# Gated cross-attention stack on one core: 16-column heads with scores formed twice

## The chip, the cores and the metric

The kernel runs on one core of a Trainium2 chip. The metric is the device time of one execution in microseconds, the median of several runs.

## The reference, cut to what matters

Four layers, each of a cross-attention and a mixture-of-experts feed-forward, work on x of shape 8 x 256 x 256 (batches, tokens, columns). The layers att1 and att2 are the ones that matter here: x is normalized, and with the context (8 x 256 x 256) it gives q, k and v of 16 heads of 16 columns. For each batch and head

```
scores = (q @ k.T) / 4 + mask        # 256 x 256
p      = softmax(scores)             # over the keys
head   = p @ v                       # 256 x 16
x      = x + tanh(g) * (concat(heads) @ Wo + bo)
```

att1 also rotates q and k (rotary positions) and is causal. In att1 the mask of keys is all ones in the data; in att2 it blanks some keys. Everything is float32. The kernel splits numbers in a rounded part (fp32r, "hi") and a remainder ("lo") where it uses the fast fp32r products: three products (hi hi, hi lo, lo hi) make one exact enough.

## The kernel before, in words

`build_program` (L2019) runs the layers one after the other; each phase ends with a barrier of all engines. `attention_layer` (L1705) calls `heads_phase` (L1032) for att1 and att2 with 16-column heads (`small`), and for att3 with 64-column heads.

A batch has 256 tokens, two tiles of 128 rows. All engines walk the same schedule: a loop over the batches (`run_loop`, the first and the last batch written out), and in it 16 slots, one for each head. In slot h, PE (L1254 to L1394) issues `scores` of head h+3, `turn_p` of head h, the rounds of this slot and `values` of head h-2:

- `scores` (L1255): a bf16 product (L1268) puts the mask in the PSUM bank, then two fp32r products of 256 columns (L1273) add q k, one for each tile of tokens. q and k are laid out in 64 rows a head, as hi and lo parts side by side, so that one product gives all parts.
- DVE takes the minimum of the negated scores (`max_of`, L1506), ACT forms the exponential with the row's minimum as its bias and sums the row (L1405), DVE inverts the sum (L1510), POOL multiplies the 128x512 weights by it (L1623).
- `turn_p` (L1280) turns the four 128x128 blocks of the weights on PE (L1284). ACT copies them to fp32r (L1412), DVE forms the remainder (L1514).
- `values` (L1287): four fp32r products of 256 columns (L1302). The stationary block has v of four heads in its columns, hi and lo, zeros elsewhere; four heads share a bank.
- `project` (L1315): the outputs of the batch, 512 rows by hi and lo, times Wo, 24 products.

The rounds prepare the next batch in two further PSUM banks: nT (turn of the normalized x, L1333), q, k, v (12 products each through `mm3`, L92, lines L94 to L96), and four rounds each of turning the laid-out q and k (L1355). POOL normalizes x (L1638, L1640), and for att1 rotates q and k (L1655 to L1663) and multiplies q by `kq` (L1666). ACT lays out the hi parts (L1436), DVE the lo parts (L1573). SP loads the next batch's context (L1244) when the v products are through. The bias is added by POOL (L1671) after DVE's L1529.

Before the loop, `load_split` (L975) runs a block of its own: DVE computes the statistics and builds the mask of every batch (L1134 to L1146), POOL clears `vp` (L1160).

## Time and profile before

| what | us |
|---|---|
| median of 3 runs | 3881.68 (3880.99 to 3884.53) |
| span of the profiled execution, first to last instruction | 3798.7 |
| median less span | 83.0 |
| PE, DVE, ACT, POOL busy | 2830.3, 2787.6, 1844.2, 1914.3 |
| mean granted TensorE clock | 0.892 of 2.4 GHz |
| att1, att2 (start to the start of the next phase) | about 412, 364 |

The profile is of one execution; its own total with launch and end is not shown beside the span. The page gives the span, each engine's busy time, the span in 40 slices, the DMA queues, the chain of work that ended last and the costliest groups by line. A group says what was written and read, shapes, count, busy time, mean ns of one, and what ended the engine's idle time before it. On PE the records of products overlap (each has a drain at its end), so the distance of two starts is what one costs.

### The profile page before, as it was taken

What the parts mean: (1) busy time and instruction counts of PE and PEld (TensorE: products, weight loads), DVE (VectorE), ACT (ScalarE), POOL (GpSimd) and SP (SyncE); (2) the same over time, 40 slices, a digit from 0 to 9 for tenths busy, and PEclk for the clock granted to TensorE, in tenths of its full rate; (3) what the DMA queues carried; (4) which work ended last, traced back from release to release, by engine and by line L of the source; (5) the groups of instructions that cost most, each with busy time, mean ns of one, the idle gap of its engine ahead of it and who ended that gap; (6) DMA issues with size and microseconds to landing.
All of it is one profiled execution on the core that took longest, in us unless ns stands there. A gap on an engine that the chain in (4) does not pass through costs nothing. (4 is left out here: it accounts for less than half of the span.)

```text
span 3798.7 us, 69506 instructions
## 1 busy us (share of the span) xinstructions
PE 2830.3 (75%) x20444; PEld 2544.2 (67%) x20480; DVE 2787.6 (73%) x5350; ACT 1844.2 (49%) x4487; POOL 1914.3 (50%) x1464
## 2 busy tenths in 40 slices
PE   5663683488969999749992588888179999598883
PEld 4562572377749999737771477777078988498883
DVE  4665697577758999868784588898656676588886
ACT  3222352266645555437772244444256666465551
POOL 0102656466623688745552666666434433227775
PEclk9786896589989999969996799999589999799997
DMA  3043685100007656420000455554300000275654
GB/s 96 17 139 121 225 248 161 41 12 17 6 28 261 210 190 208 157 72 12 11 6 29 149 156 158 158 155 129 100 8 12 6 11 6 96 238 183 188 179 131
DMA packets 244101, 410.95 MB, mean 108 GB/s; under 512 B 25952, under 2 KB 135660, under 8 KB 243680
## 3 DMA queue, kind: packets, MB, share of 16 engines
q1 hardware_dynamic: 230112, 371.43, 30.8%
q0 software_dynamic: 13824, 37.53, 3.1%
q8 instruction: 78, 1.28, 0.1%
q14 instruction: 87, 0.71, 0.1%
HBM read 330.72 MB, written 78.38 MB: 108 GB/s over the span
## 5 line engine op out<-in xcount | busy, mean ns | idle before, releaser
L1623 POOL TENSOR_TENSOR att_p<-att_p,att_ri 128x512 f32<-128x512 f32 x384 | 416.9, 1088 | 600.6 <-DVE att_ri L1510 596.7
L500 POOL TENSOR_TENSOR moe2m_wlo<-moe2m_raw,moe2m_whi 128x768 fp32r<-128x768 f32 x184 | 343.4, 1867 | 199.2 <-ACT moe2m_whi L623 166.2
L1405 ACT ACTIVATE att_p<-att_s,att_nm 128x256 f32<-128x256 f32 x768 | 357.9, 477 | 39.3 <-DVE att_nm L1506 37.9
L1514 DVE TENSOR_TENSOR att_pTlo<-att_t,att_pThi 128x512 fp32r<-128x512 f32 x384 | 263.8, 687 | 107.9 <-ACT att_pThi L1412 106.0
L500 POOL TENSOR_TENSOR moe1m_wlo<-moe1m_raw,moe1m_whi 128x768 fp32r<-128x768 f32 x138 | 273.3, 1987 | 128.7 <-ACT moe1m_whi L623 128.7
L1506 DVE TENSOR_REDUCE att_nm<-att_s 128x2 f32<-128x512 f32 x384 | 261.5, 681 | 93.9 <-PE att_s L96 45.5
L500 POOL TENSOR_TENSOR moe3m_wlo<-moe3m_raw,moe3m_whi 128x512 fp32r<-128x512 f32 x184 | 249.1, 1370 | 138.1 <-ACT moe3m_whi L623 124.7
L717 DVE TENSOR_TENSOR moe2m_hlo<-moe2m_h_f,moe2m_hhi 128x256 fp32r<-128x256 f32 x184 | 302.5, 1644 | 13.9 <-issue 0.3
L1412 ACT ACTIVATE att_pThi<-att_t 128x512 fp32r<-128x512 f32 x384 | 230.8, 601 | 157.0 <-PE att_t L1284 153.9
L1284 PE MATMUL att_t<-g_ident,att_p 128*128 128x128 f32 x1536 | 254.9, 290 | 19.6 <-POOL att_p L1623 18.3
L587 POOL DMA_INDIRECT rows_x<-moe_n_all,moe_slot_w x144 | 151.5, 1052 | 220.1 <-POOLq L109 118.0
L94 PE MATMUL moe1m_gu<-moe1m_xThi,moe1m_whi 128*128 128x256 f32 x744 | 213.7, 287 | 7.7 <-DVE moe1m_xTlo L677 7.7
L717 DVE TENSOR_TENSOR moe3m_hlo<-moe3m_act,moe3m_hhi 128x256 fp32r<-128x256 f32 x248 | 201.1, 811 | 19.6 <-issue 1.3
L651 ACT ACTIVATE moe2m_act<-moe2m_gu 128x256 f32<-128x256 f32 x184 | 70.5, 383 | 296.9 <-PE moe2m_gu L96 296.9
L1284 PEld LDWEIGHTS att_t<-g_ident,att_p 128*128 128x128 f32 x1536 | 171.4, 144 | 61.5 <-POOL att_p L1623 27.9
L94 PE MATMUL moe2m_gu<-moe2m_xThi,moe2m_whi 128*128 128x256 f32 x736 | 210.9, 287 | 1.4 <-DVE moe2m_xTlo L677 1.4
L95 PE MATMUL moe1m_gu<-moe1m_xTlo,moe1m_whi 128*128 128x256 f32 x744 | 210.9, 284 | 0.0
L96 PE MATMUL moe1m_gu<-moe1m_xThi,moe1m_wlo 128*128 128x256 f32 x744 | 210.5, 283 | 0.0
L95 PE MATMUL moe2m_gu<-moe2m_xTlo,moe2m_whi 128*128 128x256 f32 x736 | 208.9, 284 | 0.0
L96 PE MATMUL moe2m_gu<-moe2m_xThi,moe2m_wlo 128*128 128x256 f32 x736 | 208.3, 283 | 0.0
L623 ACT ACTIVATE moe1m_whi<-moe1m_raw 128x768 fp32r<-128x768 f32 x186 | 157.6, 847 | 96.6 <-PE moe1m_yp L96 75.3
L94 PE MATMUL moe2m_yp<-moe2m_whi,moe2m_hhi 128*128 128x256 f32 x368 | 121.5, 330 | 92.0 <-DVE moe2m_hlo L717 91.4
(591 smaller groups left out, 11209.0 us busy)
## 6 DMA issues: line engine op xcount, KB each, us to landing
moe1m_raw<-in_moe_w SPq DMA_DIRECT2D x186, 384.0 KB, 4.4
moe2m_raw<-in_moe_w SPq DMA_DIRECT2D x184, 384.0 KB, 3.1
moe3m_raw<-in_moe_w SPq DMA_DIRECT2D x248, 256.0 KB, 3.5
moe0m_raw<-in_moe_w SPq DMA_DIRECT2D x92, 320.5 KB, 3.5
rows_x<-att_zeros SPq DMA_DIRECT2D x24, 512.0 KB, 6.5
...
```

What stands on the lines that cost most here:

```text
L94: pe.matmul(out, lhs[0], rhs[0], start=first, stop=False, **kw)
L95: pe.matmul(out, lhs[0], rhs[1], start=False, stop=False, **kw)
L96: return pe.matmul(out, lhs[1], rhs[0], start=False, stop=last, **kw)
L500: e.tensor_tensor(wlo[s][:, :], raw[s][:, 0:WW], whi[s][:, :].bitcast(F32), ALU.subtract).then_inc(w_lo_v if in_shared(i, lo, hi, c // FC) ...
L623: act.activation(whi[s][:, :], raw[s][:, 0:WW], ACT.Copy).then_inc(w_hi, 1)
L717: v.tensor_tensor(hh[1][q][:, :], h_f[q][:, :], hh[0][q][:, :].bitcast(F32), ALU.subtract).then_inc(h_ready, 1)
L1284: mm = pe.transpose(t_ps[s % 2][:, kc, t * P:(t + 1) * P], p_sb[s % 4][:, t, kc * P:(kc + 1) * P], ident[:, :])
L1405: ins = act.activation(p_sb[s % 4][:, t, :], src[:, t, :], ACT.Exp, bias=nm[:, s % 4, t:t + 1], scale=-1.0, accum_out=rs[:, s % 4, t:t + 1])
L1412: act.activation(pT[0][s % 4][:, :, :], t_ps[s % 2][:, :, :], ACT.Copy).then_inc(ph_done, 1)
L1506: v.tensor_reduce(nm[:, s % 4, :], s_ps[s % 2][:, :, :], AX.X, ALU.min).then_inc(m_ready, 1)
L1514: v.tensor_tensor(pT[1][s % 4][:, :, :], t_ps[s % 2][:, :, :], pT[0][s % 4][:, :, :].bitcast(F32), ALU.subtract).then_inc(pl_done, 1)
L1623: pool.tensor_tensor(p_sb[s % 4][:, :, :], p_sb[s % 4][:, :, :], ri[:, s % 4, :].rearrange("p (t o) -> p t o", o=1).broadcast_to([P, TB, S ...
```

## The change

att1 and att2 get a function of their own, `small_phase`. Each head's scores are formed twice. The straight ones (`scores`, eight slots ahead) serve only to find the largest of each row (`largest` on DVE). The maxima of four heads are turned on PE (round "mt"), negated by ACT and written by two small transfers of SP into row 49 (and 113) of the laid-out q, opposite to a row of ones in k. The turned scores (`shifted`: k is stationary, q streams) then come out less the maximum; ACT's exponential (`weights_of`) writes the weights turned, into one of four fp32 buffers. `values`, two heads behind, has a weight block as stationary operand and streams 17 columns of v, the last of them ones, as a plain fp32 product; the 17th column of the result is the row's sum. `normalize` divides eight heads at a time and OT is turned on PE. q of every second head is laid out in the other 64 rows, with zeros in the rest, so the products use all 128 rows. In att1 only three of the four blocks of a head are formed (`QB` 384), the causal mask is a product of 128x128 bf16 constants, and rows that see no key get their weights by a product with `ind`. The mask of keys is a column beside the laid-out k. The loop over the batches is written out in all engines. Wo is no longer doubled (`OC` 2).

```diff
@@ lay_out, head_weights @@
-    out["L1_Wo"], out["L2_Wo"] = twice(tr(a["L1_xattn_Wo"])), twice(a["L2_xattn_Wo"])
-    out["mask2"] = a["mask_Bx1xS2_ik0"].reshape(B, S)
+    out["L1_Wo"], out["L2_Wo"] = np.ascontiguousarray(tr(a["L1_xattn_Wo"])), a["L2_xattn_Wo"]
+    by_token = lambda m: np.ascontiguousarray(m.reshape(B * TB, P).T)
+    out["mask1"], out["mask2"] = by_token(a["mask_BxS2_if1"]), by_token(a["mask_Bx1xS2_ik0"])
-    HD, OC = 16 * dh, 4 if dh == 16 else 8
+    HD, OC = 16 * dh, 2 if dh == 16 else 8
@@ new function @@
+def small_phase(nc, G, I, name, layer, weights, w, mask, biases, rotary):
+    H, dh, L = 16, 16, 8
+    NS = B * H
+    scale = 0.25
+    NEG = -1.0e9 if rotary else -BIG
+    QB = 384 if rotary else 512
+    MC = 3 if rotary else 2
+
+    plan = [(-4, "nT", 0), (-3, "q", 0), (-2, "k", 0), (1, "v", 0), (3, "qT", 0), (5, "kT", 0), (6, "qT", 1), (7, "kT", 1),
+            (8, "qT", 2), (10, "kT", 2), (11, "qT", 3), (15, "kT", 3), (13, "mt", 0), (17, "mt", 1), (21, "mt", 2), (25, "mt", 3),
+            (27, "OT", 0), (35, "OT", 1), (37, "out", 0)]
+    ROUNDS = sorted(((16 * (b - 1) + at, kind, b, part) for b in range(B) for at, kind, part in plan), key=lambda r: r[0])
+    POS = {r[1:]: i for i, r in enumerate(ROUNDS)}
...
+    def rounds_at(s):
+        return [r[1:] for r in ROUNDS if r[0] == s]
...
+        qs, ks = (sb(n, [P, TB, H, 4, dh], F32R) for n in ("qs", "ks"))
+        QT = [sb(f"QT{q}", [P, 2, H // 2, S], F32R) for q in range(2)]
+        KT = [sb(f"KT{q}", [P, H // 2, S], F32R) for q in range(2)]
+        vp = [sb(f"vp{q}", [P, KC, H, dh + 1]) for q in range(2)]
+        p_sb = [sb(f"p{q}", [P, QB]) for q in range(4)]
...
+                for s in range(FIRST, LAST):
+                    for kind, b, part in rounds_at(s):
+                        if kind == "mt":
+                            n = 4 * b + part
+                            sp.wait_ge(mt_done, n + 1)
+                            for e in range(2):
+                                sp.dma_start(QT[b % 2][64 * e + 49:64 * e + 50, e, 2 * part:2 * part + 2, :].bitcast(F32),
+                                             mT[n % 2][4 * e:4 * e + 4, :].bitcast(F32)).then_inc(row_in, 16)
+                        if kind == "v" and b < B - 1:
+                            load_c(b + 1)
...
+                def scores(s):
+                    b, h = divmod(s, H)
+                    j = h // 4
+                    if h % 4 == 0:
+                        pe.wait_ge(rd_act, done("qT", b, j))
+                        pe.wait_ge(rd_dve, done("kT", b, j))
+                    if s == H:
+                        pe.wait_ge(cleared, 2)
+                    if s >= 2:
+                        pe.wait_ge(m_done, s - 1)
+                    bank, q, k = s_ps[s % 2], QT[b % 2], KT[b % 2]
+                    if rotary:
+                        pe.matmul(bank[:, P:3 * P], ident16[:, :], tri[:, :, :], start=True, stop=False, skip_group_check=True)
+                        pe.matmul(bank[:, 0:2 * P], q[:, h % 2, h // 2, 0:P], k[:, h // 2, :], start=False, stop=False, skip_group_check=True)
+                        mm = pe.matmul(bank[:, 2 * P:3 * P], q[:, h % 2, h // 2, P:S], k[:, h // 2, 0:P], start=False, stop=True, skip_group_check=True)
+                    else:
+                        for t in range(TB):
+                            mm = pe.matmul(bank[:, t * S:(t + 1) * S], q[:, h % 2, h // 2, t * P:(t + 1) * P], k[:, h // 2, :], start=(t == 0), stop=True,
+                                           skip_group_check=True)
+                    mm.then_inc(s_ready, 1)
+
+                def shifted(s):
+                    b, h = divmod(s, H)
+                    if h % 4 == 0:
+                        pe.wait_ge(row_in, 32 * (4 * b + h // 4 + 1))
+                    if s >= 2:
+                        pe.wait_ge(e_done, s - 1)
+                    bank, q, k = t_ps[s % 2], QT[b % 2], KT[b % 2]
+                    if rotary:
+                        if s == 0:
+                            pe.wait_ge(dg_done, 1)
+                        pe.matmul(bank[:, P:3 * P], tri[:, 0, :], dg[:, b, :, :], start=True, stop=False, skip_group_check=True)
+                        pe.matmul(bank[:, 0:S], k[:, h // 2, 0:P], q[:, h % 2, h // 2, :], start=False, stop=False, skip_group_check=True)
+                        mm = pe.matmul(bank[:, S:S + P], k[:, h // 2, P:S], q[:, h % 2, h // 2, 0:P], start=False, stop=True, skip_group_check=True)
+                    else:
+                        for c in range(KC):
+                            mm = pe.matmul(bank[:, c * S:(c + 1) * S], k[:, h // 2, c * P:(c + 1) * P], q[:, h % 2, h // 2, :], start=(c == 0), stop=True,
+                                           skip_group_check=True)
+                    mm.then_inc(st_ready, 1)
+
+                def values(s):
+                    b, h = divmod(s, H)
+                    g, half = h % 8, s // 8
+                    if h == 0:
+                        pe.wait_ge(rd_dve, done("v", b))
+                    if g == 0 and half >= 2:
+                        pe.wait_ge(on_done, half - 1)
+                    out = o_ps[half % 2][:, 0:16 * (dh + 1)].rearrange("p (t h c) -> p t h c", t=2, h=8)
+                    v = vp[b % 2]
+                    if rotary and g == 0:
+                        if s == 0:
+                            pe.wait_ge(ind_done, 2)
+                        pe.matmul(out[:, 1, :, :], ind[:, b, :], v[:, 1, 8 * (h // 8):8 * (h // 8) + 8, :], start=True, stop=False, skip_group_check=True)
+                    pe.wait_ge(e_done, s + 1)
+                    p = p_sb[s % 4]
+                    if rotary:
+                        blocks = [(0, 0, 0), (1, 0, P), (0, 1, 2 * P)]
+                    else:
+                        blocks = [(t, c, c * S + t * P) for c in range(KC) for t in range(TB)]
+                    for i, (t, c, at) in enumerate(blocks):
+                        mm = pe.matmul(out[:, t, g, :], p[:, at:at + P], v[:, c, h, :], start=(not rotary and g == 0 and i == 0),
+                                       stop=(i == len(blocks) - 1), skip_group_check=True)
+                    mm.then_inc(pv_done, 1)
+
...
+                    elif kind in ("qT", "kT"):
+                        if part == 0:
+                            pe.wait_ge(aux_done, b + 1)
+                            pe.wait_ge(laid_lo, 2 * b + 1 + (kind == "kT"))
+                        flat = (qs if kind == "qT" else ks)[:, :, :, :, :].rearrange("p t h g d -> p t (h g d)")
+                        for c in range(2):
+                            for t in range(TB):
+                                at = c * S + (1 - t if kind == "qT" else t) * P
+                                mm = pe.transpose(bank[:, at:at + P].bitcast(F32R), flat[:, t, (2 * part + c) * P:(2 * part + c + 1) * P], identr[:, :])
+                    elif kind == "mt":
+                        n = 4 * b + part
+                        pe.wait_ge(mq_ready, n + 1)
+                        mm = pe.transpose(bank[0:8, 0:P], mm_sb[n % 2][:, :, :, :].rearrange("p e a t -> p (e a t)"), ident[:, :])
...
+                pe.wait_ge(cleared, 1)
+                for s in range(FIRST, max(LAST, NS + 3)):
+                    if rotary and s == -7:
+                        pe.wait_ge(dg_done, 1)
+                        for q in range(2):
+                            pe.matmul(o_ps[q][:, :], G["ones_bf"][:, :], dgc[:, 4 * q:4 * q + 4, :], start=True, stop=True).then_inc(ind_ready, 1)
+                    if 0 <= s + L < NS:
+                        scores(s + L)
+                    if 0 <= s < NS:
+                        shifted(s)
+                    for r in rounds_at(s):
+                        round_(*r)
+                    if 0 <= s - 2 < NS:
+                        values(s - 2)
...
+                def weights_of(s):
+                    act.wait_ge(st_ready, s + 1)
+                    if s >= 4:
+                        act.wait_ge(pv_done, s - 3)
+                    act.activation(p_sb[s % 4][:, :], t_ps[s % 2][:, 0:QB], ACT.Exp).then_inc(e_done, 1)
+
+                def lay_hi(b, kind):
+                    f, dst = (qf, qs) if kind == "q" else (kf, ks)
+                    act.wait_ge(f_ready, 2 * b + 1 + (kind == "k"))
+                    if b > 0:
+                        act.wait_ge(rd_ready, POS[(kind + "T", b - 1, 3)] + 1)
+                    src = f[:, :, :].rearrange("p t (h d) -> p (t h) d", d=dh)
+                    flat = dst[:, :, :, :, :].rearrange("p t h g d -> p (t h) g d")
+                    src = src.rearrange("p n (o d) -> p n o d", o=1).broadcast_to([P, TB * H, 2, dh])
+                    act.activation(flat[:, :, 0:2, :] if kind == "q" else flat[:, :, 0:3:2, :], src, ACT.Copy).then_inc(laid_hi, 1)
...
+                    elif kind == "qT":
+                        act.wait_ge(rd_ready, pos + 1)
+                        if b >= 2:
+                            act.wait_ge(st_ready, 16 * (b - 2) + 4 * part + 4)
+                        for e in range(2):
+                            ins = act.activation(QT[b % 2][64 * e:64 * e + 64, e, 2 * part:2 * part + 2, :], both(bank)[64 * e:64 * e + 64], ACT.Copy)
+                        ins.then_inc(rd_act, 1)
+                    elif kind == "mt":
+                        n = 4 * b + part
+                        act.wait_ge(rd_ready, pos + 1)
+                        if n >= 2:
+                            act.wait_ge(row_in, 32 * (n - 1))
+                        act.activation(mT[n % 2][:, :], bank[0:8, 0:P], ACT.Copy, scale=-1.0)
+                        act.drain().then_inc(mt_done, 1)
+                        act.drain().then_inc(rd_act, 1)
...
+                def largest(s):
+                    b, h = divmod(s, H)
+                    n, e, a = s // 4, h % 2, h % 4 // 2
+                    v.wait_ge(s_ready, s + 1)
+                    if h % 4 == (3 if rotary else 0) and n >= 2:
+                        v.wait_ge(rd_ready, POS[("mt", (n - 2) // 4, (n - 2) % 4)] + 1)
+                    m = m3 if rotary else mm_sb[n % 2]
+                    v.tensor_reduce(m[:, e, a, :], s_ps[s % 2][:, 0:QB].rearrange("p (c k) -> p c k", c=MC), AX.X, ALU.max).then_inc(m_done, 1)
+                    if h % 4 == 3:
+                        if rotary:
+                            v.drain()
+                            v.tensor_tensor(mm_sb[n % 2][:, :, :, 0], m3[:, :, :, 0], m3[:, :, :, 1], ALU.max)
+                            v.tensor_copy(mm_sb[n % 2][:, :, :, 1], m3[:, :, :, 2])
+                        v.drain().then_inc(mq_ready, 1)
+
+                def lay_lo(b, kind):
+                    f, dst = (qf, qs) if kind == "q" else (kf, ks)
+                    v.wait_ge(laid_hi, 2 * b + 1 + (kind == "k"))
+                    src = f[:, :, :].rearrange("p t (h d) -> p (t h) d", d=dh)
+                    flat = dst[:, :, :, :, :].rearrange("p t h g d -> p (t h) g d")
+                    lo, hi = (2, 0) if kind == "q" else (1, 0)
+                    v.tensor_tensor(flat[:, :, lo, :], src, flat[:, :, hi, :].bitcast(F32), ALU.subtract).then_inc(laid_lo, 1)
...
+                def normalize(half):
+                    b, g = divmod(half, 2)
+                    v.wait_ge(pv_done, 8 * half + 8)
+                    if half >= 2:
+                        v.wait_ge(rd_ready, POS[("OT", b - 1, g)] + 1)
+                    o = o_ps[half % 2][:, 0:16 * (dh + 1)].rearrange("p (n c) -> p n c", c=dh + 1)
+                    v.reciprocal(ri[:, :], o[:, :, dh])
+                    v.drain()
+                    out = o_sb[:, :, g * P:(g + 1) * P].rearrange("p t (h d) -> p t h d", d=dh)
+                    o4 = o_ps[half % 2][:, 0:16 * (dh + 1)].rearrange("p (t h c) -> p t h c", t=2, h=8)
+                    r4 = ri[:, :].rearrange("p (t h o) -> p t h o", t=2, o=1).broadcast_to([P, 2, 8, dh])
+                    v.tensor_tensor(out, o4[:, :, :, 0:dh], r4, ALU.mult).then_inc(on_done, 1)
...
+                def aux(b):
+                    if b > 0:
+                        pool.wait_ge(rd_ready, POS[("kT", b - 1, 3)] + 1)
+                    for t in range(TB):
+                        cols = lambda y: y[:, TB * b + t:TB * b + t + 1].broadcast_to([P, H])
+                        if rotary:
+                            pool.tensor_copy(qs[:, t, :, 3, 0], kq[:, b, t:t + 1].broadcast_to([P, H]))
+                        pool.tensor_copy(ks[:, t, :, 3, 0], cols(km))
+                    pool.drain().then_inc(aux_done, 1)
...
+                def clear(q):
+                    for e in range(2):
+                        pool.drain()
+                        pool.memset(QT[q][64 - 64 * e:128 - 64 * e, e, :, :].bitcast(F32), 0.0)
...
+                pool.wait_ge(stats, 1)
+                norm(0)
+                clear(0)
+                pool.drain().then_inc(cleared, 1)
+                pool.wait_ge(kq_done, 1)
+                for b in range(B):
+                    if b > 0:
+                        norm(b)
+                    aux(b)
+                    if rotary:
+                        rotate(b, "q")
+                        rotate(b, "k")
+                    if b == 0:
+                        clear(1)
+                        pool.drain().then_inc(cleared, 1)
+                    if b >= 2:
+                        add_bias(b - 2)
...
@@ attention_layer @@
-        heads_phase(nc, G, I, "att1", 1, 16, head_sources(I, 1), w, mask=I["mask_BxS2_if1"], rotary=True,
-                    biases=(I["L1_bq"], I["L1_bk"], I["L1_bv"]))
+        small_phase(nc, G, I, "att1", 1, head_sources(I, 1), w, I["mask1"], (I["L1_bq"], I["L1_bk"], I["L1_bv"]), True)
     if layer == 2:
-        heads_phase(nc, G, I, "att2", 2, 16, head_sources(I, 2), w, mask=I["mask2"],
-                    biases=(I["L2_xattn_bq"], I["L2_xattn_bk"], I["L2_xattn_bv"]))
+        small_phase(nc, G, I, "att2", 2, head_sources(I, 2), w, I["mask2"], (I["L2_xattn_bq"], I["L2_xattn_bk"], I["L2_xattn_bv"]), False)
     if layer == 3:
```

## Rows read from the trace of the kernel before

**Rows 1.** Windows of att1 and att2: stretch, busy us (instructions) of each engine, PEclk, DMA, GB/s

```profile
680.00:1092.00 412.00, 337.08 (x2140) 276.07 (x2176) 283.05 (x612) 250.47 (x800) 237.90 (x225) 0.87 0.05 15
1641.00:2005.00 364.00, 325.81 (x2176) 262.69 (x2176) 276.07 (x601) 251.14 (x801) 176.05 (x153) 0.93 0.05 16
```

**Rows 2.** Timeline of SP: issues of the context loads, two of att1, two of att2

```profile
765.02 0.35 SPq L1244 DMA_DIRECT2D att_cT_hi<-ctxT_hi  x1
...
991.50 0.33 SPq L1244 DMA_DIRECT2D att_cT_hi<-ctxT_hi  x1
...
1704.76 0.34 SPq L1244 DMA_DIRECT2D att_cT_hi<-ctxT_hi  x1
...
1909.54 0.33 SPq L1244 DMA_DIRECT2D att_cT_hi<-ctxT_hi  x1
```

**Rows 3.** Timeline of PE, one head of att2: start, us covered, line, operation

```profile
1695.59 0.39 PE L1268 MATMUL att_s<-att_mask,att_ident 128*128 128x512 bf16 x1
...
1696.34 0.66 PE L1284 MATMUL att_t<-g_ident,att_p 128*128 128x128 f32 x4
1696.75 0.37 PE L1302 MATMUL att_o<-att_pThi,att_vp 128*128 128x256 f32 x1
1696.96 0.28 PE L1302 MATMUL att_o<-att_pTlo,att_vp 128*128 128x256 f32 x1
1697.08 0.28 PE L1302 MATMUL att_o<-att_pThi,att_vp 128*128 128x256 f32 x1
...
1697.32 0.39 PE L1268 MATMUL att_s<-att_mask,att_ident 128*128 128x512 bf16 x1
```

**Rows 4.** Timeline of PE in att1: four turns of laid-out q

```profile
993.33 0.54 PE L1355 MATMUL att_r<-g_identr,att_qs 128*128 128x128 f32 x4
```

**Rows 5.** Groups of att2 by line and shape: count, busy us, mean ns, idle before

```profile
L1506 DVE TENSOR_REDUCE att_nm<-att_s 128x2 f32<-128x512 f32 x128 | 87.0, 680 | 22.8 <-PE att_s L1273 19.5 <-issue 2.6 <-ACT att_p L1405 0.6
...
L1412 ACT ACTIVATE att_pThi<-att_t 128x512 fp32r<-128x512 f32 x128 | 77.1, 602 | 43.4 <-PE att_t L1284 41.4
```

**Rows 6.** Timeline of PE in the router of the second expert phase (fp32 products, turns)

```profile
1105.28 3.60 PE L274 MATMUL moe1r_lgp<-moe1r_nT,moe1r_rw 128*8 128x512 f32 x8
1108.81 0.41 PE L280 MATMUL moe1r_small<-g_ident,moe1r_lgT 8*128 8x8 f32 x4
```

**Rows 7.** Timeline of the start of att1

```profile
680.51 4.36 POOL L1160 MEMSET att_vp<- 128x5120 f32 x1 [8.86 <-POOLq L109]
...
690.65 2.77 DVE L1141 TENSOR_TENSOR att_mask<-att1p_causal,att1p_row 128x512 bf16<-128x512 bf16 x8
693.49 4.42 DVE L1144 TENSOR_REDUCE att_kq<-att_mask 128x16 f32<-128x4096 bf16 x1
...
701.68 1.12 PE L1333 MATMUL att_r<-g_ident,att_n 128*128 128x128 f32 x4 [96.20 <-POOLq L1647]
...
707.97 1.29 POOL L1655 TENSOR_TENSOR att_turn<-att_qf,att_cs 128x512 f32<-128x512 f32 x1 [6.47 <-DVEq L1545]
...
713.23 1.06 ACT L1436 ACTIVATE att_qs<-att_qf 128x1024 fp32r<-128x1024 f32 x1 [9.80 <-POOL att_qf L1666]
...
729.60 0.79 PE L1273 MATMUL att_s<-att_KT,att_QT 64*128 64x256 f32 x2 [0.38 <-DVE att_QT L1555]
```

**Rows 8.** Timeline of PE: the wait of att1 behind the rotation of q

```profile
1031.03 0.61 PE L1268 MATMUL att_s<-att_mask,att_ident 128*128 x1 [3.23 <-ACT att_p L1405]
```

**Rows 9.** Timeline of PE: start of att2

```profile
1655.28 1.12 PE L1333 MATMUL att_r<-g_ident,att_n 128*128 128x128 f32 x4 [62.95 <-POOLq L1647]
...
1672.99 0.65 PE L1268 MATMUL att_s<-att_mask,att_ident 128*128 128x512 bf16 x1
```

**Rows 10.** The context load by its line: issue to landing, us

```profile
DMA to landing us min/median/max: 2.5/2.8/3.2
```

**Rows 11.** Windows of a start of att2 and of an end of att1 (as rows 1)

```profile
1680.00:1688.00 8.00, 8.00 (x29) 5.55 (x29) 4.76 (x10) 4.92 (x17) 5.87 (x6) 0.50 0.01 2
1062.00:1082.00 20.00, 18.02 (x119) 13.96 (x119) 15.58 (x36) 16.53 (x55) 11.72 (x12) 1.00 0.01 1
```

261 lines of the change are left out of this document (259 added, 2 removed).

## The prediction

> **What bounds the kernel now.** I read the windows of the two phases first. The change touches only the two attention phases with 16-column heads: att1 (rotary, causal), about 412 us, and att2, about 364 us [rows 1]. In both, PE has work for 80 to 90% of the time, DVE and ACT for two thirds, so no engine waits for memory; the loads of the context are two per batch. Those loads mark the batches, because the next one is issued when the v projection is through: five batches of att1 take 991.50 - 765.02 = 226.5 us, 45.3 each, five of att2 1909.54 - 1704.76 = 204.8 us, 41.0 each [rows 2].
>
> Then the PE timeline of one warm head in att2 [rows 3]. It goes from mask to mask in 1697.32 - 1695.59 = 1.73 us: the bf16 mask product and the two score products 0.75, the four turns of the weights 0.41, the four value products 0.57. Back-to-back products of 256 columns are 0.12 apart (1696.96 to 1697.08); the first after turns costs 0.21, so a switch of kind costs about 0.09. Sixteen heads are 27.7 us. A round of four fp32r turns covers 0.54, of which the drain of the last is 0.16 (0.28 long at a pitch of 0.12), so it holds PE for 0.38 [rows 4]. Rounds of a batch now: nT 0.4, q, k, v 36 x 0.12 = 4.3, eight turns 3.0, output 24 x 0.12 = 2.9, together 10.6. Work of PE: 38.3 of 41.0 us. So att2 is bound by PE; att1 adds about 4 us of waits.
>
> **The change, part by part.** *Removed per head:* on PE the mask product, the four turns (0.41) and the four wide value products (0.57); on ACT two exponentials with their accumulator reads and the copy of 0.60; on DVE the subtraction of 0.69 and the reciprocal; on POOL the normalization. *Kept:* the maximum, 0.68 us on DVE; ACT now does one exponential of 128x512 from PSUM, for which I take the copy of that shape, 0.60 [rows 5]. PE now writes the scores twice, straight and turned.
>
> *Scores in att2:* 4 x 0.12 = 0.48. *Values:* four fp32 products of 17 columns with a full stationary block. The trace has no such thing. The nearest: an fp32 product appears as two records (the router's 8 records in 3.60 us are four products, 0.43 a record for 512 columns, two cycles a column) [rows 6]. So each value product is two loads and two short streams. The same group has four fp32 loads of 128 columns, each followed by 8 columns: 0.41 us in all, less 0.16 of drain, 0.06 each; without taking off the drain 0.10. I take 0.07, near the lower end since 17 columns at two cycles are 14 ns. Eight of them: 0.56, with bounds 0.48 and 0.83. The Trainium skill (TensorE: Matmul & The Clock Gate, LDWEIGHTS) puts a load at columns/1.2 ns, 107 ns for 128; by it the eight would be 0.86. The row above, 0.10 at most, speaks against it. A head is then 0.48 + 0.56 + 0.09 (one switch) = 1.13, sixteen 18.1 us.
>
> *Rounds:* output 12 products instead of 24 (1.4), OT turns 0.4, mt turns 0.4, the rest as before: 9.5, and 0.9 for ten switches: 10.4. Sum 28.5. The gap between work and batch is 2.7 us now; v no longer waits behind the doubled layout on DVE, so I keep 2.1: **30.6 us a batch in att2**. The cover is good: ACT has 16 x 0.60 + about 9.9 (the four qT copies in two halves 4.8, layouts 2.1, the rest 3) = 19.5; DVE 16 x 0.68 + about 10.5 = 21.4.
>
> *att1:* each set of scores is a bf16 product of 256 columns (0.11), one fp32r of 256 (0.12) and one of 128 (0.10): 0.65 for both. Values 6 x 0.07 = 0.42, the product for empty rows 0.03, three switches 0.3: 1.40 a head, 22.4 the batch, with rounds 32.8. Now a stall. POOL fills the auxiliary columns for batch b only when kT of batch b-1 is through, one slot before ACT lays out q. The q rotation takes from 707.97 to 713.23, 5.2 us, and k one multiplication less, about 4.2 [rows 7]. With the fill it is 6 us after the start of that slot, and ACT wants it after about 2. Behind that wait on ACT sit the next exponentials, behind the layout on DVE the maxima, and PE's scores wait for those. Counting on through both layouts PE loses about 3.4 us a batch. Now it loses 3.2 in one such wait and the clock falls after it [rows 8]; I add 3 us for that: **39.2 us a batch in att1**.
>
> *Prologue of att1:* the mask operations on DVE go (2.77 and 4.42 us), and with them a block boundary and casts, some 2 us; PE would start its first turns at 692.5 instead of 701.68. Added: zeroing half of QT before PE may start. The memset of 5120 columns takes 4.36, so 2 x 2048 take 3.5; in att1 that lies beside DVE's small mask operations and costs nothing, in att2, where DVE has less to lose, it costs what the boundary gives. Rotation, layouts and eight heads' scores ahead of the first turned ones put slot 0 at about 725; now the first scores are at 729.60 [rows 7]. att2: PE starts at 1655.28 and has scores at 1672.99 [rows 9]; then follow eight heads' scores, the next batch's nT, q and k and the first maxima, so slot 0 comes at about 1681.
>
> *The row of maxima:* PE turn, ACT copy and drain, then two small transfers of SP. A load of the context lands 2.5 to 3.2 us after issue [rows 10]; for 2 KB I take 2.0 (bounds 1.5 and 3.2). In all about 3.7 us; from the turn to the first use there are two and a half slots with their rounds, 4.3 or more. Cost nothing; if late, 1 us four times a batch.
>
> **The sum.** att1: 45 + 7 x 39.2 + last batch 25 (16 x 1.40 and 2.8 of rounds) + tail 7 = 351, now 412: -61. att2: 40 + 7 x 30.6 + 21 + 7 = 282, now 364: -82. Four small weight blocks less in the two preceding expert phases cost and give nothing, they lie beside the gathers. The span 3798.7 us becomes 3656; the median 3881.68 is 83 us more than the span (launch and end, the profiled execution's own total isn't shown), so 3739, rounded **3740 us**.
>
> **Rivals.** *Loads bound the values.* A stationary load is not hidden and a pair costs 0.104 as in the turns (four in 0.41) [rows 3]. Then +0.27 a head in att2 and +0.20 in att1: 128 x 0.47 = 60 us, 3800. This is what the skill's LDWEIGHTS rule says as well. For: the load has nothing long to hide behind. Against: rows 6. Chance 0.15.
>
> *Late row of maxima, or waits at each hand-over:* four waits of 1 us in 16 batches, 64 us: 3804. For: SP issues in order, two transfers each. Against: the distance in slots. Chance 0.13.
>
> *Everything better hidden:* no switches, no stall: batches of 26.5 and 31 us, -29 and -57: 3655. Against: switches are in the rows, and the wait for the rotation too. Chance 0.12.
>
> *Slower: the clock.* In 1680 to 1688 PE is busy for 8.00 of 8.00 us and the granted clock stays 0.50 (1.2 GHz), with many turns in the mix; in 1062 to 1082 it is 1.00 (2.4 GHz) [rows 11]. The skill (same page, PE-mode transpose) says that turns don't count as busy for the gate; the first row fits, and by that rule dropping them costs nothing. But value products that are mostly loading may weigh as little. At half clock a head of att2 is 4 x 0.21 + 8 x 0.14 + 0.1 = 2.1 us and its rounds about 17: 51 a batch, +20; att1 +18. Over all batches 38 x 7.5 = 285 us, 4025. It decides from half: 143 of 285. I put the case at 0.65 of the time: +185, 3925. For: about 45% of a warm head streams columns, where now 46% does beside the turns, so it is close. Against: q, k, v and output are dense and bring it back. Chance 0.12.
>
> **Numbers.** Forecast case 0.48, its own range 3690 to 3790. The range takes in all but the clock case: 3640 to 3860. About 0.2% (8 us) can be told from no change. Faster 0.87 (all but the clock case and a little), within 0.2% 0.02, slower 0.11.
>
> **What would show it.** Right: batches of 31 and 39 us between context loads; fp32 value records about 0.07 apart; POOL in att1 ending its rotation while ACT waits in the layout; clock near 1.0 in att2. Wrong: value pairs at 0.10; PE waiting for the row's DMA; a granted clock of 0.5 between the dense rounds; a batch of att1 over 45.

## The result, and the profile after

The changed kernel takes 3955.15 us (median of 4 runs, 3950.98 to 3963.29) where the kernel before takes 3881.34 in the same set: ratio 1.0196, 95% interval 1.0181 to 1.021. It is 74 us slower; the forecast was 3740. (Of the experiments below, one of the four executions of turned_stand_longer took 5655.61 us, for a reason that nothing here shows, and its ratio is that of the other three.)

Busy times and the clock, from the page of the profile after:

```profile
span 3952.3 us, 66552 instructions
...
PE 2920.9 (74%) x20707; PEld 2736.4 (69%) x20708; DVE 2545.5 (64%) x4818; ACT 1616.1 (41%) x3415; POOL 1638.4 (41%) x1281
...
PEclk9776896666667999967665699999689999799997
```

ACT, DVE and POOL lost what the change takes from them (ACT 1844 before, DVE 2788, POOL 1914). PE did not, and its granted clock is at 5 to 7 tenths in both changed phases (slices 8 to 12 and 18 to 22 of the 40), where the kernel before had 8 or 9 in most.

The windows of single batches after, from context load to context load (columns: stretch, its length, PE busy and records, granted clock, DMA share, GB/s); they answer to [rows 1]:

```profile
804.80:856.10 51.30, 43.87 (x292) 0.67 0.03 12
...
1785.80:1827.20 41.40, 38.72 (x287) 0.84 0.04 14
1827.20:1878.50 51.30, 48.88 (x286) 0.63 0.04 12
1878.50:1929.80 51.30, 48.89 (x286) 0.63 0.04 11
```

The first batch of att2, from the same kind of view, is another matter:

```profile
1755.60:1785.80 30.20, 29.97 (x268) 1.00 0.06 19
```

It takes 30.2 us at the upper level of the clock (2.4 GHz). That it lies so near the 30.6 of the forecast is luck: it has 268 records of PE where the later ones have 286, since no earlier batch is there whose output products and second turn of sums it would carry. A full batch at this clock takes 32.5 us (ot_later_repeat, below). Then something takes the clock away: 41.4, 51.3, 51.3, 51.3. In att1 the last four batches take 51.2 each. So the work is 2 us a batch above the forecast, and the rest of the time is made by the clock.

PE timeline of one head's values at the upper and at the lower level:

```profile
1776.20 0.96 PE L1871 MATMUL att_o<-att_vp,att_p 128*128 128x17 f32 x8
1777.01 0.49 PE L1828 MATMUL att_s<-att_KT,att_QT 128*128 128x256 f32 x2
...
1902.09 1.85 PE L1871 MATMUL att_o<-att_vp,att_p 128*128 128x17 f32 x8
1903.77 0.77 PE L1828 MATMUL att_s<-att_KT,att_QT 128*128 128x256 f32 x2
```

Eight records (four fp32 products, two records each) take 1777.01 - 1776.20 = 0.81 us, 0.10 for each load with its stream, and 1.68 at the lower level (1.2 GHz), 0.21 each. I had taken 0.07, with 0.10 as the upper bound.

PE's timeline at the point where the clock falls, and DVE's beside it:

```profile
1787.49 0.40 PE L1847 MATMUL att_t<-att_QT,att_KT 128*128 128x256 f32 x2
1789.64 0.41 PE L1918 MATMUL att_r<-g_ident,att_o 128*128 128x128 f32 x2 [1.75 <-DVE att_o L2043]
1789.81 0.54 PE L1910 MATMUL att_r<-g_identr,att_qs 128*128 128x128 f32 x4
1790.18 1.72 PE L1871 MATMUL att_o<-att_vp,att_p 128*128 128x17 f32 x8
```

```profile
1788.13 0.69 DVE L2030 TENSOR_TENSOR att_ks<-att_kf,att_ks 128x512 fp32r<-128x512 f32 x1 [0.79 <-ACT att_ks L1962]
1788.74 0.25 DVE L2038 RECIPROCAL att_ri<-att_o 128x16 f32<-128x16 f32 x1
1789.07 0.42 DVE L2043 TENSOR_TENSOR att_o<-att_o,att_ri 128x256 f32<-128x256 f32 x1
```

PE wants to turn the second half of the sums (round OT, part 1). It stands 1.75 us, because DVE's division (L2038, L2043) comes behind DVE's part of the layout of k (L2030), which waits 0.79 us for ACT's part. Ahead of the wait eight value records take 0.81 us, behind it (1790.18 to the next scores at 1791.75) 1.57. A wait of this length comes once a batch, and the others are shorter; the waits of PE in 224 us of att2 (us in total, times, longest), and in four batches of att1:

```profile
PE att_r L1918 <- DVE att_o L2043: 7.4, 6, 1.8
PE att_r L1910 <- DVEq L2077: 2.7, 4, 0.8
```

```profile
PE att_r L1918 <- DVE att_o L2043: 14.0, 4, 3.5
PE att_s L1823 <- DVE att_m L2016: 13.1, 4, 3.3
```

The clock also fell once without such a wait. In the batch of 41.4 us it had come back, and fell again behind a wait of 0.17 us (PE's timeline, then windows; their columns are PE, PEld, DVE, ACT and POOL busy, clock, DMA share, GB/s):

```profile
1809.15 0.41 PE L1918 MATMUL att_r<-g_ident,att_o 128*128 128x128 f32 x2 [0.17 <-DVE att_o L2043]
```

```profile
1800.00:1810.00 10.00, 9.83 (x91) 9.64 (x91) 5.93 (x10) 6.25 (x13) 1.07 (x2) 1.00 0.00 1
1810.00:1820.00 10.00, 10.00 (x61) 9.93 (x61) 3.89 (x6) 3.61 (x7) 0.00 (x0) 0.66 0.01 2
```

No run explains this second fall.

No wait for the row of maxima shows in either phase. In att1 the same turn waits 3.5 us and the scores 3.3: both stand behind layouts that wait for the rotation. ACT's waits of the same four batches of att1:

```profile
ACT att_qs L1962 <- POOL att_qf L2155: 20.8, 4, 5.2
...
ACT att_ks L1962 <- POOL att_kf L2151: 8.7, 4, 2.2
```

### The profile page after: what moved, and what is told of

Same layout as the page of the kernel before. It is cut to its first block and busy times, and to the rows that moved or that the text cites. A ratio compares the mean times of both kernels' runs of the same rounds, so it can differ in the third digit from the quotient of the medians.

```text
span 3952.3 us, 66552 instructions
## 1 busy us (share of the span) xinstructions
PE 2920.9 (74%) x20707; PEld 2736.4 (69%) x20708; DVE 2545.5 (64%) x4818; ACT 1616.1 (41%) x3415; POOL 1638.4 (41%) x1281
## 5 line engine op out<-in xcount | busy, mean ns | idle before, releaser
L1871 PE MATMUL att_o<-att_vp,att_p 128*128 128x17 f32 x1792 | 326.0, 317 | 0.0
L1871 PEld LDWEIGHTS att_o<-att_vp,att_p 128*128 128x128 f32 x1792 | 325.4, 269 | 0.7
L1952 ACT ACTIVATE att_p<-att_t 128x384 f32<-128x384 f32 (+1 forms) x256 | 138.9, 542 | 388.9 <-PE att_t L1847 210.7
L717 DVE TENSOR_TENSOR moe2m_hlo<-moe2m_h_f,moe2m_hhi 128x256 fp32r<-128x256 f32 x184 | 284.8, 1548 | 14.1 <-issue 0.6
L1623 POOL TENSOR_TENSOR att_p<-att_p,att_ri 128x512 f32<-128x512 f32 x128 | 132.8, 1040 | 290.9 <-DVE att_ri L1510 289.2
L94 PE MATMUL moe3m_yp<-moe3m_whi,moe3m_hhi 128*128 128x256 f32 x496 | 149.4, 301 | 56.2 <-DVE moe3m_hlo L717 49.1
L715 DVE CAST moe1m_hhi<-moe1m_h_f 128x256 fp32r<-128x256 f32 x186 | 173.7, 934 | 15.6
L2016 DVE TENSOR_REDUCE att_mm<-att_s 128x2 f32<-128x512 f32 x128 | 88.2, 689 | 126.3 <-PE att_s L1828 125.0
```

The costliest lines, as they stand in the source:

```text
L94: pe.matmul(out, lhs[0], rhs[0], start=first, stop=False, **kw)
L715: v.tensor_copy(hh[0][q][:, :], h_f[q][:, :])
L717: v.tensor_tensor(hh[1][q][:, :], h_f[q][:, :], hh[0][q][:, :].bitcast(F32), ALU.subtract).then_inc(h_ready, 1)
L1623: pool.tensor_tensor(p_sb[s % 4][:, :, :], p_sb[s % 4][:, :, :], ri[:, s % 4, :].rearrange("p (t o) -> p t o", o=1).broadcast_to([P, TB, S ...
L1871: mm = pe.matmul(out[:, t, g, :], p[:, at:at + P], v[:, c, h, :], start=(not rotary and g == 0 and i == 0), stop=(i == len(blocks) - 1), s ...
L1952: act.activation(p_sb[s % 4][:, :], t_ps[s % 2][:, 0:QB], ACT.Exp).then_inc(e_done, 1)
```

## The experiments

Eighteen runs were made, in six sets, each set on one chip (those with the same time of before in the table). On three chips the kernel before takes 3880 to 3883 us, on the three others 3796 to 3802; so ratios are compared, not times, across sets. "Batches" are steady ones, in us between context loads.

```
run                  median   before   ratio (95% interval)     att1 batches   att2 batches
before_again         3880.64  3880.11  1.0001 (0.9991-1.0011)   45.1 to 45.5   40.6
filler_1             3927.28  3880.11  1.0114 (1.0085-1.0143)   44.6 to 57.8   41.1 to 56.5
filler_2             3901.36  3880.11  1.0067 (1.0042-1.0092)   47.2 to 47.7   41.9 to 46.5
values_single        3741.96  3880.11  0.9650 (0.9631-0.9669)   38.2 to 39.4   31.2 to 37.3
filler_narrow        4077.98  3882.16  1.0513 (1.0484-1.0541)   43.6 to 55.2   65.2 to 67.2
aux_late             3907.59  3882.16  1.0067 (1.0041-1.0092)   37.4 to 49.1   51.2
single_aux_late      3720.85  3882.16  0.9588 (0.9568-0.9607)   35.1 to 38.7   32.5 to 37.2
single_filler        3759.38  3882.16  0.9669 (0.9649-0.9689)   40.7 to 41.1   32.7 to 42.3
turned_fp32          3761.69  3883.39  0.9683 (0.9667-0.9699)   36.7           34.7
turned_single        3682.38  3883.39  0.9486 (0.9469-0.9504)   33.0 to 34.0   28.5
single_ot_later      3682.41  3883.39  0.9499 (0.9450-0.9548)   32.0 to 33.3   27.5 to 29.1
fp32_ot_later        3678.99  3801.43  0.9685 (0.9663-0.9706)   35.2 to 36.4   32.5
ot_later_repeat      3656.50  3795.86  0.9642 (0.9618-0.9667)   35.2 to 36.5   32.5
after_repeat         3872.89  3795.86  1.0205 (1.0188-1.0222)   51.2 to 54.4   51.3
ot_later_only        3719.08  3795.86  0.9781 (0.9739-0.9823)   39.9 to 49.5   32.5
stand_put_back       3711.76  3795.86  0.9768 (0.9743-0.9793)   35.2 to 45.5   33.6 to 45.7
stand_longer         3791.16  3801.57  0.9963 (0.9937-0.9989)   36.3 to 45.5   44.3 to 48.7
turned_stand_longer  3736.57  3801.57  0.9829 (0.9809-0.9849)   36.7           41.0 to 41.6
```

**before_again.** The kernel before, unchanged.

> The kernel before, unchanged, profiled a second time. Its first profiled execution has a span of 3798.7 us while the runs have a median of 3881; I took the 83 us for launch and end. In the changed kernel the span is 3952.3 of 3954.4, so that cannot be. Expected: total within 3 us of the span, near 3880, and against the first profile the extra time in phases that the change does not touch (the expert phases), att1 and att2 batches again 45.3 and 41.0 us between context loads. If instead the batches of att1 and att2 are longer here, the forecast started from wrong durations as well.

Span 3878.8 of a total of 3880.65: only 2 us lie around the span. The batches are 45.3 and 40.6, where the first profile has 45.3 and 41.0. The 80 us more lie where the change is not: the window of the second expert phase takes 465.00 us here and 442.30 in the profile before, the fourth 455.90 and 427.00, and the first ends 22 us later. The windows (columns: PE, PEld, DVE, ACT, POOL busy, clock, DMA share, GB/s), first of the profile before, then of before_again:

```profile
1149.70:1592.00 442.30, 440.37 (x3467) 422.05 (x3468) 406.16 (x632) 247.90 (x428) 299.25 (x162) 1.00 0.61 203
```

```profile
1175.50:1640.50 465.00, 447.86 (x3466) 426.83 (x3467) 405.68 (x632) 247.67 (x428) 296.37 (x162) 0.97 0.58 193
```

So my "83 us around the span" was wrong in kind, though not in what it did to the sum: the forecast's difference stands.

**filler_1, filler_2.** More work in each head: the first product of each group once more (filler_2: twice more), here for att2's scores; the turned scores and the bf16 products of att1 likewise.

```
-                        for t in range(TB):
+                        for t in [0] * 1 + [0, 1]:
```

> The changed kernel with more work: in every head the first product of each of the two groups of scores is issued once more into the same place (256 more columns each, 512 a head; the second overwrites the first). Theory A (the clock): the granted clock is at its lower level because PE mostly loads weights between the dense rounds, and more streamed columns bring it back. Then a batch of att2 takes 31.5 + 16 x 0.24 = about 35 us instead of 51.3, one of att1 about 45 instead of 51.2, together some 140 us less: 3815. A half effect (clock up in part of the stretches): 3880 to 3950. Theory B (the loads and waits alone, the clock follows from elsewhere): every head 0.4 to 0.5 us longer at the lower clock, 16 batches x 7 = 110 us more: 4065. Theory C (the late rotation lets the clock fall): att2, which has no rotation, would stay at 51 plus 7.

> As filler_1, but the first product of each group is issued three times (1024 more columns a head, 0.48 us at the upper clock, 0.85 at the lower). Theory A: the clock at its upper level through almost all of att2; a batch of att2 35 + 4 = 39 us, of att1 about 49: 3870. If filler_1 already holds the clock, filler_2 is 16 x 16 x 0.24 = 61 us slower than it; if filler_1 does not and this one does, it is faster than filler_1. Theory B: 220 us slower than the changed kernel, 4175.

More work made it faster: 28 and 54 us less than the 3955 of the change. Two batches of filler_2 in att2:

```profile
1768.50:1810.50 42.00, 39.95 (x351) 1.00 0.05 14
1810.50:1857.00 46.50, 44.45 (x350) 0.89 0.04 13
```

51.3 us had become 41.9 to 46.5 with 0.48 us a head added. A sum of waits and loads alone would have grown; it is the clock that makes the loss. How much of it comes back I had too high: filler_1 alternates in att2 (41.1, 56.5) and its total is that of the half effect, and filler_2 takes 3901 where 3870 was expected. att2 has no rotation, so a late rotation alone (theory C) is out for that phase. The longer slots also shorten the wait at the second turn, from 1.75 to 1.28 us, so these two runs do not part the wait from the columns. In the batch of 42.0 us the clock held behind it:

```profile
1772.98 0.41 PE L1920 MATMUL att_r<-g_ident,att_o 128*128 128x128 f32 x2 [1.28 <-DVE att_o L2045]
```

**filler_narrow.** The same extra products with 16 columns instead of 256.

> Control for filler_2: again two more products in each group of scores, four a head, with the same stationary block loaded each time, but each streams 16 columns instead of 256. Theory A (streamed columns bring the clock back, loads do not): the clock stays low at least as long as in the changed kernel, each pair costs 0.21 us at the lower clock, 0.84 a head, 13 a batch: batches of 60 us and more, in all 3955 + 150 to 215 = 4105 to 4170. Theory A2 (it is the number of products, or any extra work between the waits, that matters): the clock rises as in filler_2 and the time is at or below 3955.

att2: 65 us a batch at a clock of 0.57 to 0.58, as expected. Its wait at the second turn is shorter still, at most 1.2 us, and the clock stays down all the same, so it is neither the number of products nor the shorter wait that brings the clock back in filler_2. att1 was a miss: three of five batches took 43.6 to 43.8 at 0.85, better than without the filler, and the total is under the 4105 to 4170 expected. I have no measured reason for that.

**values_single.** The weights (p), the values and the table for empty rows in fp32r, one load and one stream a product; what is left out is the precision of these operands below fp32r.

```
-        vp = [sb(f"vp{q}", [P, KC, H, dh + 1]) for q in range(2)]
-        p_sb = [sb(f"p{q}", [P, QB]) for q in range(4)]
+        vp = [sb(f"vp{q}", [P, KC, H, dh + 2], F32R) for q in range(2)]
+        p_sb = [sb(f"p{q}", [P, QB], F32R) for q in range(4)]
```

> The changed kernel with weights, values and the table for empty rows in fp32r instead of fp32, so that each value product is one load and one stream instead of two of each (this leaves precision out of the weights and the values). Both theories want it faster; the clock tells them apart. Theory A: fewer loads between the scores, the clock comes back for most of att2: head 1.37 - 0.41 = 0.96, batch 15.4 + 10 = 25 us, att1 stall-bound near 42; together 3955 - 7 x 26 - 7 x 9 = about 3700. Theory B (clock stays low): head 2.68 - 0.84 = 1.84 us, batch 51.3 - 13.4 = 38 us in att2 and 51.2 - 10 = 41 in att1, 3785. If a single-pass load takes as long as the two of fp32, no change: 3955.

138 us faster than the kernel before, between the 3700 and the 3785 of the two theories, with batches of 31.2 to 37.3 us in att2. A head's values take 0.37 us (1771.48 to 1771.85 in its PE timeline) for 0.81. But PE stands more, since it has less to do:

```profile
1744.54 0.41 PE L1918 MATMUL att_r<-g_ident,att_o 128*128 128x128 f32 x2 [2.20 <-DVE att_o L2043]
```

and the clock still falls after that wait (0.89 over a batch of 32.4 us). Here I should have seen it; I read it as a wait of 2 us and no more.

**aux_late, single_aux_late, single_filler.**

```
-                    aux(b)
                     if rotary:
                         rotate(b, "q")
                         rotate(b, "k")
+                    aux(b)
```

> The changed kernel with one call moved on POOL: the auxiliary columns are filled behind the two rotations instead of ahead of them, so that the rotation of batch b no longer waits for the last turned keys of batch b-1. ACT now waits 5.2 us for the rotated q and 2.2 for k in every batch of att1. If the late rotation is a cause of its own: 3 to 5 us less in each of 7 batches and perhaps a shorter stretch at the lower clock, 3955 - 30 = 3925. If the wait is covered by PE's work at the lower clock: 3950 to 3955. att2 must stay as it is, batches of 51.3.

> values_single (3742) with the same move on POOL. Here PE has less work a batch (38.5 us in att1), so the wait for the rotation weighs more: 4 to 5 us in 7 batches, 3742 - 32 = 3710. If the move only shifts the wait to the turned q, where the auxiliary columns are needed: 3735 to 3745.

> values_single with the extra products of filler_1 (512 more columns a head). In values_single the clock is still low in a third of att2, batches are 25.6 us where it is high and 32 where it falls. Theory A: with 0.24 us more a head the clock holds; batches of 29 to 30 in att2, 3 less than now, att1 about as now: 3720 to 3742. If values_single is not held back by the clock any more: 16 batches x 4 = 64 us more, 3806.

The order on POOL is a cause of its own in att1: batches of 37.4 and 38.6 (clock 0.91 and 0.87) beside 46 and 49 (0.71 and 0.65), 48 us in all, more than the 30 expected. PE's wait of 3.3 us at the scores is gone; the one at the second turn is left, up to 3.4 us. att2 did not move (51.2). With the single products the gain is 21 us, where 32 was expected. single_filler is 17 us slower than values_single: neither the +64 of "clock settled" nor a gain.

**turned_fp32, turned_single.** The value windows become the stationary operand and the weights stream, in att2 one product per chunk of keys; the sums are copied, turned in two more rounds a batch and divided after that. Core of the diff:

```
+                    out = o_ps[half % 2][:, S * (g // 4):S * (g // 4) + S]
+                    win = lambda c: vp[b % 2][:, c, h // 4, P * (h % 4):P * (h % 4) + P]
...
-                        mm = pe.matmul(out[:, t, g, :], p[:, at:at + P], v[:, c, h, :], start=(not rotary and g == 0 and i == 0),
-                                       stop=(i == len(blocks) - 1), skip_group_check=True)
+                        mm = pe.matmul(dst, win(c), rhs, start=(g == 0 and i == 0), stop=(i == len(blocks) - 1), skip_group_check=True)
```

> aux_late with the values product turned round, all still in fp32: the value windows (zero-padded to 128 columns, four heads stacked 32 rows apart) are the stationary side, the weights stream with 256 columns; the sums are copied by DVE, turned by PE in two more rounds a batch, and divided after that. Streaming costs twice two records of about 0.22 us a head, as much as the eight short pairs at the upper clock (0.88 against 0.81), plus 0.8 us of turns a batch. By work alone a batch of att2 is then 1 to 2 us longer at any given clock: 52 to 53 us if the clock stays low. Theory A (the clock needs streamed columns): four loads a head instead of eight, and 1024 columns at two cycles; the clock holds and a batch of att2 takes 16 x 1.46 + 11.2 = 35 us, one of att1 about 43: 3907 - 90 = about 3810.

> The same in fp32r (precision left out of weights and values as in values_single): two products of 256 columns a head. Theory A: head 0.56 + 0.24 + 0.09, batch 14 + 11 + 2 to 4 of waits = 28 us in att2 where single_aux_late has 32.5 to 37, about 35 in att1 as there, limited by the rotation: 3720 - 35 = 3685. If the two added rounds wait (copy, turn, division in a row on DVE) 2 us twice a batch: 3740.

Batches of 34.7 and 28.5 us in att2, as expected to half a microsecond; in att1 36.7 and 33 to 34, where 43 and 35 were expected. A window of turned_fp32:

```profile
1735.30:1770.00 34.70, 33.07 (x230) 1.00 0.05 16
```

Another miss: the four wide records stand 1740.31 - 1739.63 = 0.68 us ahead of the next scores, not 0.88. The scores behind them take some 0.1 us more, so that a head goes from 1735.16 to 1736.50, in 1.34 us, where one with the narrow products takes 1.37 (1785.80 to 1787.17): by work the two forms are nearly the same. I took the result for proof that the loads bring the clock down. But the kernel also carried aux_late's order and later slots for the turns, so one more control ran.

**single_ot_later, fp32_ot_later, ot_later_repeat, after_repeat, ot_later_only.** One line of the plan:

```
-            (27, "OT", 0), (35, "OT", 1), (37, "out", 0)]
+            (28, "OT", 0), (36, "OT", 1), (38, "out", 0)]
```

> single_aux_late with the turns of the sums and the output product one slot later (28, 36 and 38 for 27, 35 and 37). PE stands 2.2 us (att2) to 4 us (att1) in each batch at the second of these turns, because DVE's division sits behind its part of the layout of k. If the wait is real work order: 2 to 3 us in 16 batches and, where PE standing still is what lets the clock fall, a little more: 3721 - 40 = 3680. If DVE is late by more than a slot or the wait only moves to the output product: 3710 to 3725.

As expected: 3682, 38 us less than single_aux_late, in one slot's difference.

> Control for turned_fp32, which besides the turned product has aux_late's order on POOL and its turns of the sums later by one slot or more: aux_late (fp32, small value products) with the turns of the sums and the output at 28, 36 and 38, as in single_ot_later. Theory A (loads and streamed columns set the clock): att2 stays low in most of each batch, 51.3 less the 2 to 3 us of the wait, 48 to 51, total 3907 - 30 = 3880. Rival (PE standing still at the second turn is what lets the clock fall): with the wait gone the clock holds, att2 batches of 32 to 35 as in turned_fp32, total about 3760.

The rival won. The same small fp32 products, loads and all, hold the clock for the whole of att2 once PE no longer stands at the second turn. The view of PE's waits is empty for five batches of att2, in this run and in its repeat. Since this run fell on a chip with a faster kernel before, it was repeated beside the unchanged change.

> fp32_ot_later once more, beside the unchanged changed kernel on the same chip, since its first run fell on a chip on which the kernel before takes 3801 and not 3881 us. If the clock holds because of the edit: ratio to the kernel before again 0.968, att2 batches of 32.5 us at the upper clock. If it held because of the chip: att2 batches near 50 here, ratio near 1.0.

> The changed kernel again, on the same chip as the three others of this set: ratio 1.02 to the kernel before, batches of 51.2 and 51.3 us. Anything below 1.01 would say that the chips differ in this.

> The changed kernel with the slots of the second turn alone (28, 36, 38), the auxiliary columns where the change put them. Theory S (PE standing at the second turn lets the clock fall, and the loading products don't bring it back): in att2, where the order on POOL plays no part, batches of 32.5 us as in fp32_ot_later; in att1 the wait for the rotation remains, 5 us on ACT, so PE still stands for 3 us there: batches of 44 to 51. Total 3955 - 110 to 150 = 3805 to 3845 on a chip where the kernel before takes 3881. If att2 stays at 51, the order on POOL was the cause, though att2 has no rotation.

Batches of att2 on one chip, first after_repeat, then ot_later_repeat:

```profile
1715.90:1746.10 30.20, 29.95 (x268) 1.00 0.06 19
1746.10:1797.50 51.40, 48.99 (x286) 0.63 0.03 11
```

```profile
1633.20:1665.70 32.50, 32.38 (x286) 1.00 0.06 18
```

The same 286 PE records; 51.4 us with a wait of 1.75 us in them, 32.5 without. ot_later_only, the change with nothing but this line, goes from 1.0205 to 0.9781: 154 us on this chip, for three numbers in a plan; a little better than expected (3805 to 3845 of 3881, that is 0.980 to 0.991). In its att1 PE still waits 3.3 us at the scores; the batches take 39.9 to 49.5 us at clocks of 0.84 to 0.64.

**stand_put_back, stand_longer, turned_stand_longer.** The wait put back by itself, in att2 alone, without work for PE; the scratch tile has 4096 columns, in the two longer ones 6144:

```
+                    if (kind, part) == ("qT", 1) and not rotary:
+                        pe.wait_ge(late, b + 1)
...
+                        pool.wait_ge(rd_ready, POS[("kT", b, 0)] + 1)
+                        pool.memset(scratch[:, :], 0.0)
+                        pool.drain().then_inc(late, 1)
```

> fp32_ot_later with a wait put in on purpose, in att2 alone: once a batch, ahead of the second round of turned queries, PE waits for a 128x4096 memset that POOL begins after the first round of turned keys (about 3.5 us, of which PE has 1.5 of other work: it stands for about 2 us). No work is added to PE. Theory S: the clock falls as in the changed kernel, batches of 45 to 51 us for 2 us of wait; total 3761 + 8 x 13 to 17 = 3865 to 3900 where before is 3881. Theory A (loads and columns alone): 34.5 us a batch, 2 us for 2 us: 3777.

> stand_put_back with the memset half longer (6144 columns), so that PE stands about 1.7 us longer in each batch of att2, 2.8 us in all. There the wait was 0.9 us in most batches and two of six fell to the lower clock (44.5 and 45.7 us against 33.6). Theory S: now most or all batches fall, 47 to 52 us: 3712 (before at 3796) + 100 = 3810. Theory A: 35.3 us a batch, 14 more in all: 3726.

> The same wait put into turned_fp32, where the weights stream with 256 columns and only four loads stand beside them. Its batch is 34.7 us at the upper clock. Theory S with A (a wait is needed and a mix poor in streamed columns behind it): the clock comes back at once or holds, 34.7 + 2.7 = 37.5 us a batch, ratio 0.968 + 0.006. Theory S alone (any wait of this length lets it fall and stay): 50 us and more, as in stand_longer.

The first four batches of att2 in stand_put_back:

```profile
1619.00:1663.60 44.60, 42.26 (x268) 0.69 0.04 13
1663.60:1697.20 33.60, 32.55 (x286) 1.00 0.05 17
1697.20:1730.80 33.60, 32.56 (x286) 1.00 0.06 18
1730.80:1776.50 45.70, 44.77 (x286) 0.70 0.04 13
```

```profile
1627.82 0.50 PE L1914 MATMUL att_r<-g_identr,att_qs 128*128 128x128 f32 x4 [2.34 <-POOLq L2199]
...
1673.51 0.51 PE L1914 MATMUL att_r<-g_identr,att_qs 128*128 128x128 f32 x4 [0.92 <-DVEq L2081]
...
1740.75 0.51 PE L1914 MATMUL att_r<-g_identr,att_qs 128*128 128x128 f32 x4 [0.91 <-DVEq L2081]
```

In the first batch the wait is 2.34 us and the clock falls. In the others it is 0.9, less than half of the 2 expected (the view names DVE as what ended it, but the same work of DVE makes no wait in ot_later_repeat, and POOL's memset ends at 1706.95, just ahead of the turn at 1707.14): it costs 1.1 us in three of four (the last not shown, 33.6 us), and 13 in the one in which the clock falls. The total, 3712, is therefore below the 3865 to 3900 forecast, the more so as before is 3796 on this chip. Which batch falls no run explains.

stand_longer, where PE stands 2.62 us at that place (its timeline, second fence): every batch falls, to 44.3 to 48.7 us, a little less than the 47 to 52 expected.

```profile
1674.30:1723.00 48.70, 46.05 (x287) 0.68 0.04 12
1723.00:1770.40 47.40, 44.74 (x286) 0.71 0.04 12
```

```profile
1686.00 0.72 PE L1914 MATMUL att_r<-g_identr,att_qs 128*128 128x128 f32 x4 [2.62 <-POOLq L2199]
```

turned_stand_longer carries the same edit before products that stream 256 columns, and PE stands even longer there, 23.3 us in six waits by the view of waits (a window, then that row):

```profile
1704.10:1745.40 41.30, 35.82 (x230) 0.92 0.04 14
```

```profile
PE att_r L1913 <- POOLq L2221: 23.3, 6, 4.1
```

41.3 for 34.7: some 6.5 us for waits of 3.9, where the small products pay 12 to 16 for one of 2.6. Less the wait itself, the clock costs 2.7 us a batch there and 9 to 14 here. So both count. The clock fell in one of four batches behind a wait of 0.9 us and in every batch behind one of 2.6, and the products that follow decide how much the fall costs. My figure of 37.5 was too low, since the waits were longer than the 2.7 I had counted on.

## Why the prediction was wrong

*The step that failed: the price of a wait.* I had counted 2.1 us of waits a batch in att2, and priced them at their length. They were there, at 1.75 us plus 0.7. Their price is 51.3 - 32.5 = 19 us a batch. [Rows 8] has such a wait of 3.23 us, and the windows behind it in the kernel before show the clock falling:

```profile
1031.00:1034.00 3.00, 2.76 (x9) 1.70 (x10) 2.50 (x4) 1.93 (x6) 2.80 (x4) 0.50 0.00 0
1034.00:1038.00 4.00, 4.00 (x21) 3.60 (x21) 1.94 (x4) 2.24 (x6) 2.69 (x3) 0.66 0.00 0
1038.00:1042.00 4.00, 3.84 (x30) 3.18 (x30) 3.70 (x9) 3.56 (x14) 1.21 (x2) 1.00 0.00 0
```

I priced that fall at 3 us in att1 and at nothing in att2. The kernel before is back at 1.00 after some 7 us; it streams columns for 0.57 us of each head's values. The changed one mostly loads, and behind its wait of 1.76 us at 1831 it is not back until about 1870:

```profile
1832.00:1867.00 35.00, 34.34 (x168) 33.73 (x169) 11.82 (x19) 11.66 (x23) 2.34 (x3) 0.50 0.01 1
```

*The rival of the clock had the right mechanism and the wrong trigger.* The case of the clock gave 2.1 us a head at the lower level and 51 us a batch; the trace has 51.3. But I made it depend on the mix of loads and columns alone, argued that q, k, v and the output would bring the clock back, and gave it 0.12. They do bring it back, late in the batch, and the next wait takes it away. With the mix alone (att2 of ot_later_repeat, no wait of PE) the clock is 1.00.

*Values: 0.07 a pair, measured 0.10.* This is 8 x 0.03 x 16 = 3.8 us a batch; 30.6 - 2.1 + 3.8 = 32.3, and the batch without waits is 32.5. The rest of the sum for att2 (scores, switches, rounds) holds. The Trainium skill (TensorE: Matmul & The Clock Gate, LDWEIGHTS) gives a load as columns/1.2 ns, 107 ns for 128 columns; the trace is near it, with 101 ns for a load and its stream of 17 columns together. I had weighed it against four tiny loads of the router and took the wrong one.

*att1: the rotation.* Forecast a stall of 3.4 us a batch and 3 us for the clock; ACT waits 5.2 and 2.2, PE 3.3 at the scores and 3.5 at the turn, so the waits of PE are twice the stall. Moving the fill behind the rotations took the best batch from 51.2 to 37.4, at a clock of 0.91; the forecast of 39.2 had a stall in it that is partly gone there.

*The row of maxima* cost nothing, as forecast: PE does not wait for it in the windows above. No run shows the 2.0 us that I took for its transfers. In a faster kernel, single_ot_later, PE does wait for it, 1.2 us in three waits of att2.

*The sum.* From the last product of an expert phase to the first of the next it was to be 61 and 82 us less. These are the rows of att1's two ends, for before_again and then for the kernel after (the last figures are the first and the last start):

```profile
L94 PE MATMUL moe0m_yp<-moe0m_whi,moe0m_hhi x184: 277/303/582, 369.9 to 627.2; 128*128 128x256 f32 x184
L94 PE MATMUL moe1m_gu<-moe1m_xThi,moe1m_whi x744: 277/283/582, 1175.5 to 1637.7; 128*128 128x256 f32 x186
```

```profile
L94 PE MATMUL moe0m_yp<-moe0m_whi,moe0m_hhi x184: 277/320/582, 367.5 to 623.0; 128*128 128x256 f32 x184
L94 PE MATMUL moe1m_gu<-moe1m_xThi,moe1m_whi x744: 276/283/582, 1199.6 to 1661.8; 128*128 128x256 f32 x186
```

548.3 became 576.6, 28 us more in att1; the same marks around att2 give 536.7 and 591.1, 54 more. Together 82, where the medians differ by 74. Against the forecast that is 89 us in att1 and 136 in att2. With the later turns and POOL's order the total comes out at the forecast after all: 0.9642 to 0.9685 of 3881 is 3742 to 3759. That is luck in part: a batch of att2 takes 2 us more than forecast and one of att1 3 to 4 less, because the stall is partly gone.

The Trainium skill (same page, A second HAM failure mode: psum-queue depth-cycling) says of a bf16 kernel that frequent short idle times of PE between groups of products make its clock go up and down. This case's trace agrees that a short wait is enough, and differs in the rest: it is fp32, the wait of 1.75 us comes once a batch, and the time is lost in the products behind it, which take 1.57 us for 0.81.

*A better kernel.* turned_single (0.9486) and single_ot_later (0.9499) beat the kernel before by 5% with fp32r weights and values (which leaves precision out), and are not told apart by their intervals; with fp32 throughout it is fp32_ot_later and turned_fp32, 3.2 to 3.6%.
